# A graph network's second layer: weighted one-hots built by one comparison and one multiplication for four columns at once

## What is computed

```python
rel_w = jnp.einsum('rb,bio->rio', w_comp, weight)      # 8 relations
xw = jnp.einsum('ni,rio->rno', x, rel_w)
msg = xw[etypes, src] * norm                           # norm: one weight per edge
node_repr = jax.ops.segment_sum(msg, dst, num_segments=x.shape[0])
return jax.nn.relu(node_repr + h_bias)
```

## Time and profile before

| | us |
|---|---|
| time, median of 3 runs | 4172.07 |
| lowest and highest | 4169.52, 4172.36 |
| span of the profiled execution | 5935.9 |
| of it before the first gather | 78.5 |
| layer 0, first gather to last | 78.5 to 3291.9 |
| layer 1, first gather to last | 3384.6 to 5916.2 |

### The profile page before, as it was taken

How to read it: one execution, slowest core, us unless ns; L and a number is a source line. 1 busy time by engine, 2 the same in 40 slices (tenths; PEclk the granted TensorE clock), 3 DMA queues, 4 the chain that set the end, 5 groups by cost and what they waited for, 6 DMA issues and landing times.

```text
span 5935.9 us, 56570 instructions
## 1 busy us (share of the span) xinstructions
PE 2543.7 (43%) x11571; PEld 1919.2 (32%) x11572; DVE 1618.6 (27%) x4105; ACT 590.2 (10%) x1461; POOL 2977.3 (50%) x3193
## 2 busy tenths in 40 slices
PE   6555555445445555555454523333332332233323
PEld 5443443333333433333333322222222222222222
DVE  3222222222222322222222322223222222322323
ACT  2111111111111111111121200000000000000000
POOL 4455554544434444443434166665656555555554
PEclk7677676766666666666666555555555555555555
DMA  4411111111111111111111111111111111111111
GB/s 84 34 29 29 32 28 36 29 23 39 26 34 35 27 35 37 34 34 36 24 43 23 44 23 23 22 23 23 22 22 23 23 22 22 22 23 21 23 22 21
DMA packets 243962, 173.98 MB, mean 29 GB/s; under 512 B 127029, under 2 KB 179500, under 8 KB 243524
## 3 DMA queue, kind: packets, MB, share of 16 engines
q0 software_dynamic: 100096, 102.60, 9.7%
q1 hardware_dynamic: 142546, 67.57, 4.8%
q10 hardware_dynamic: 882, 0.13, 0.0%
HBM read 136.38 MB, written 33.70 MB: 29 GB/s over the span
## 4 chain that ended last, share of the span: by engine, by line
issue 34%; DVEq 20%; another core or an unknown queue 17%; PE 15%; DVE 12%; ACT 2%; ACTq 0%; DMA 0%; POOL 0%; POOLq 0%; SPq 0%
DVEq L879 5%; PE ps_agg L1217 4%; DVE work L936 3%; DVEq L936 3%; PE ps_fin L1289 3%; PE ps_o L1209 3%; DVEq L899 3%; DVEq L898 2%; DVE hid L948 2%; DVEq L913 2%; PE ps_z L1197 2%; PE ps_o L1205 1%; ACT acc L681 1%; DVE work L955 1%
## 5 line engine op out<-in xcount | busy, mean ns | idle before, releaser
L555 POOL DMA_INDIRECT rows<-node_table,src_ix x1564 | 1478.7, 945 | 1739.0 <-DVE work L955 1206.0
L555 POOL DMA_INDIRECT rows<-rel_table,src_ix x1564 | 1477.0, 944 | 1147.3 <-issue 460.3
L936 DVE TENSOR_SCALAR work<-ps_x,rel,enorm 128x128 f32<-128x128 f32 x1564 | 552.4, 404 | 912.7 <-issue 905.9
L1205 PE MATMUL ps_o<-b2e,ones 3*128 3x256 bf16 x391 | 134.6, 344 | 1379.2 <-DVE hid L948 1154.8
L1217 PE MATMUL ps_o<-work,rows 128*64 128x128 f32 x1248 | 291.4, 410 | 854.5 <-DVE work L936 529.0
L1217 PE MATMUL ps_agg<-work 128*64 128x128 f32 x3128 | 571.5, 342 | 47.5 <-issue 45.9
L899 DVE TENSOR_TENSOR acc<-acc,ps_agg 64x128 f32 x548 | 152.4, 278 | 1566.8 <-remote 981.8
L1217 PEld LDWEIGHTS ps_o<-work,rows 128*64 128x64 f32 x1248 | 234.3, 215 | 910.3 <-DVE work L936 555.4
L1205 PEld LDWEIGHTS ps_o<-b2e,ones 3*128 3x128 bf16 x391 | 37.4, 96 | 1485.9 <-DVE hid L948 1203.8
L1217 PEld LDWEIGHTS ps_agg<-work 128*64 128x64 f32 x3128 | 455.6, 175 | 154.1 <-issue 147.2
L1217 PE MATMUL ps_agg<-work,rows 128*64 128x128 f32 x1256 | 291.8, 412 | 342.8 <-DVE work L936 212.2
(11 more groups left out here) (137 smaller groups left out, 1905.6 us busy)
## 6 DMA issues: line engine op xcount, KB each, us to landing
rows<-node_table,src_ix POOLq DMA_INDIRECT x1564
rows<-rel_table,src_ix POOLq DMA_INDIRECT x1564
attr<-in_edge_attr_dram SPq DMA_DIRECT2D x78, 320.0 KB
rel_table<-acc SPq DMA_DIRECT2D x13, 1792.0 KB, 6.6
node_table<-work SPq DMA_DIRECT2D x24, 128.0 KB, 2.0
out_dram<-x_sb SPq DMA_DIRECT2D x13, 224.0 KB
rel_table<-acc SPq DMA_DIRECT2D x7, 256.0 KB, 2.0
src_ix<-row_groups SPq DMA_DIRECT2D x78, 10.0 KB
```

Of the source, the lines that this page charges most:

```text
L555: nc.gpsimd.indirect_dma_start(rows[0:n, slot_of(u), j, :], None, table, bass.IndirectOffsetOnAxis(ap=src_ix[0:n, half_of(u), col : col + ...
L936: last = nc.vector.tensor_scalar(o[:, j, :], iota_ps, r[:, j : j + 1], weights[:, j : j + 1], ALU.is_equal, ALU.mult)
L1205: nc.tensor.matmul(ps_o[u % 2][:, 0 : J * F], ones_3[:], b2e_3[:], start=True, stop=False, skip_group_check=True)
```

## The change

Layer 1's one-hots of a tile are made in two steps, each over 128x512 elements. `mark1` compares, with the same `one_hot` that layer 0 uses, and lifts a new semaphore `hot_marked`. `weigh1` waits for it, multiplies the tile's one-hots in place by the weights in `enorm`, repeated along the 128 places, and lifts `hot_ready`. `weigh1` of a tile stands behind `mark1` of the tile after it. So when VectorE gets to the sum of tile u, tile u+4 is marked and tile u+3 is weighted. The rare extra windows of a tile (`extras`) still use `weighted_hot`.

```diff
-            def prepare1(i, u):
-                s = tile_of(i, u)
-                weighted_hot(onehot[:, u % AHEAD, :, :], rel_of(s), s).then_inc(hot_ready, 1)
+            def mark1(i, u):
+                one_hot(onehot[:, u % AHEAD, :, :], rel_of(tile_of(i, u))).then_inc(hot_marked, 1)
+
+            def weigh1(i, u):
+                hot = onehot[:, u % AHEAD, :, :]
+                weights = enorm[:, bass.ds(tile_of(i, u), 1), :].rearrange("p o (j n) -> p (o j) n", n=1)
+                dve.wait_ge(hot_marked, tile_of(i, u) + 1)
+                nc.vector.tensor_tensor(hot, hot, weights.to_broadcast([P, J, P]), ALU.mult).then_inc(hot_ready, 1)
...
-            for u in range(AHEAD - 1):
-                prepare1(0, u)
+            mark1(0, 0)
+            for u in range(1, AHEAD - 1):
+                mark1(0, u)
+                weigh1(0, u - 1)
             with dve.Fori(0, BODIES - 1) as i:
                 for u in range(BODY):
-                    prepare1(i, u + AHEAD - 1)
+                    mark1(i, u + AHEAD - 1)
+                    weigh1(i, u + AHEAD - 2)
                     add_supertile1(i, u)
```

More of the change, by code:

```diff
@@ L281, in bass_gnn_resnorm_d2_kernel @@
         msg_ready = sem("msg_ready")
+        hot_marked = sem("hot_marked")
         hot_ready = sem("hot_ready")
@@ L1094, in _ @@
                 if u + AHEAD - 1 <= BODY:
-                    prepare1(BODIES - 1, u + AHEAD - 1)
+                    mark1(BODIES - 1, u + AHEAD - 1)
+                if u + AHEAD - 2 <= BODY:
+                    weigh1(BODIES - 1, u + AHEAD - 2)
                 add_supertile1(BODIES - 1, u, u == BODY)
```

## The result

The changed kernel takes 4207.60 us (median of 4 runs, 4201.21 to 4215.24) against 4172.22 us (4 runs, 4169.52 to 4174.0). The ratio is 1.0089, with a 95% interval of 1.0077 to 1.0101. The forecast was 4244 us, slower.

What follows compares the result with a forecast made beforehand. POOL's gathers were taken to bound both layers, at 5.0 us a tile. VectorE's work and the added wait cost 0 and collisions 72 us, so 4172 + 72 = 4244 us, range 4170 to 4330 us.

Steps and rivals of the forecast that it cites:

- The sum of POOL's steps: Both layers: 3127 gather steps of 1.249 us plus start, ring, between-layer and end terms, 4143.7 us, 0.7% below measured.
- The full ring: Layer 0's start: POOL fills the ring before the first message is made, 48.5 us more than a step.
- The long steps of 2.45 us: POOL's gathers: steps twice as long without a wait; one in every 80 gathers would be 47 us.
- The pace of 0.70 us: VectorE's sequencer in layer 1: about 0.70 us an instruction in slow stretches, taken as an effect of the recording.
- VectorE's own part: Layer 1: two instructions, together 1.37 us, replace four of 1.36 us; about 2.4 us a tile beside POOL's 5.0, cost 0.
- The added wait and the lag: Layer 1: wait on `hot_marked` met before reached, one-hots ready three tiles ahead instead of four; cost 0.
- The collision: Layer 1: the two-SBUF-input multiplication holds gathers at their reading point, 0.185 us a tile, 72 us; chance 0.72.
- the free phase: Layer 1: multiplication falls freely in POOL's 1.249 us step; collision chance 0.54, mean wait 0.34 us.
- No collision: Rival, layer 1: the weighings miss POOL's reading points or the held gather had another cause; 4172 us, chance 0.16.
- the whole length lost: Rival, layer 1: each multiplication costs POOL its full 0.68 us, 266 us, giving 4438 us; chance 0.08.
- Faster: Rival: VectorE bounds parts of layer 1, so fewer instructions bring back up to 28 us, 4144 us; chance 0.04.
- the gather at 2021.08: POOL's gather started 0.15 us after L1009 (SBUF with SBUF): 1.29 us instead of 0.945, 0.34 us lost.

Runs made afterwards that it cites:

- 128x768 between: The changed kernel with an idle 128x768 multiplication, one input in PSUM, between comparison and multiplication in the loop: 4211.19 us, ratio 1.0105.
- 128x256 between: The changed kernel with an idle 128x256 multiplication, one input in PSUM, between comparison and multiplication in the loop: 4176.82 us, ratio 1.0027.

## Why the prediction was right, and where not

**What bounds the kernel: right in layer 1, with a wrong reason, and in layer 0 partly by luck.** The sum of POOL's steps came to 4144 us. On a chip that isn't paced the terms can now be read, in the changed kernel: 79.4 us ahead of the first gather (78.5 assumed), 93.7 between the layers (92.7), 17.3 from the last gather's start (19.7). Layer 1 takes 1992.7 us from first to last start, that is 1563 steps of 1.249 us, 1952.2, and 40.5 more, which is what the held gathers lost. In layer 0 two errors partly cancel. The full ring cost 20.7 us more than a step and not the 48.5 that were read from the paced profile:

```profile
151.77 0.94 POOL L556 DMA_INDIRECT rows<-node_table,src_ix  x1 [20.98 <-DMA src_ix<-src_groups]
```

In its place seven later waits of POOL in layer 0, of 1.3 to 17.3 us, five of them put down to row numbers, cost 52.7 us beyond the usual step, and the sum had none of them. What is left of the two, 25 us, is most of the 28 us that the sum lacked. So layer 0 isn't bound by POOL's steps alone. These seven waits are about as large in the kernel before with the PSUM multiplication added (48.4 us), so they have nothing to do with the change. The long steps of 2.45 us, offered for the missing 28 us, don't appear there as a series: layer 1 has none. The pace of 0.70 us was put down to the recording. It goes with the chip that the run falls on: there all executions of the kernel before take 5839 to 5958 us, while profiles from the other chips don't show it. What causes it stays open. The waits that it makes were rightly left out for the chips of 4170 us, and would have been wrongly left out for the others.

**VectorE's own part at cost 0: right.** The comparison took 691 ns and the multiplication 682, as taken from L889 and L863. The run with the added multiplication from PSUM shows that 0.7 us a tile more on VectorE is free (ratio 0.9995).

**The added wait and the lag at cost 0: not refuted.** `hot_marked` shows up in no wait. The run without the lag fell on paced chips, so the lag's own price at POOL's pace was not measured; since 41.8 us of lost gathers stand against 35.4 us of lost time, there is hardly room for one.

**The collision: right in kind, too large in size.** This was the term that carried the forecast, read from one case in one trace, and 123 cases followed it. The term was 0.185 us a tile, 72 us; measured were 0.107 us, 41.8 us in the gathers and 35.4 us in the time, half of the forecast. It was mis-sized in two places:
- The hold was taken as long as the instruction's record, 0.68 us. It lasts 0.555. The earlier trace rows would have told: the gather was let go about 0.50 us after a 448-column instruction began, 0.13 us before its record ended. I had laid that 0.13 us on the gather's side, as the time until it reads; the lengthened multiplications at a gather's start show that it reads within some 0.05 us. With 0.555 us the free phase gives 391 x 0.555² / (2 x 1.249) = 48 us.
- The phase was taken as free. It is not: 31% of the multiplications held a gather, by 0.34 us, where a free phase would have 44%, by 0.28. Fewer collisions, each a little longer, left 42 of the 48 us. That they came so near to the free phase is luck: the run with 128x256 between lost 14 us.

**The rivals.** No collision and the whole length lost are out, the second because a gather that is past its start is seldom held, and 0.107 us a tile is far from 0.68. Faster is out: nothing came back. One argument for the collision was misread: of the four long gathers before 97 us none has VectorE reading SBUF "with both hands". Three ran beside casts, with one tensor input, and one beside a clearing, with none. Only the gather at 2021.08 ran beside an instruction with two SBUF inputs, so it alone bore the term. What the Trainium skill's "SBUF — State Buffer" says in "Who interferes with whom" of two SBUF inputs against a reading GpSimd instruction agrees with the runs here that had two SBUF inputs, and with the two that read one of them from PSUM and held nothing. That the later of the two is blocked shows both ways, in the 123 held gathers and in the 13 lengthened multiplications, but the gather was let go 0.13 us before the multiplication's record ended. The section infers that a `tensor_tensor` doesn't hold up the making of descriptors. For these gathers it can't be concluded from this that the multiplication is free: 57.4 us were lost in the run with the added multiplication in SBUF. Whether the reading of the row numbers or the making of the descriptors is held, no run here tells apart.

**The profile's signs.** A mean of 0.99 us was expected, 0.970 came; single gathers of up to 1.6 us, 1.458 came. Layer 0's mean stayed at 945 ns. The fall of the profiled span from 5936 to 4210 us came with the chip as far as the runs can tell, and says nothing for or against what was said of it.

## What to carry to other kernels

When POOL issues indirect DMAs back to back and is the bound, an instruction of VectorE is only free if it leaves POOL alone: keep one of two tensor inputs in PSUM, as the run that marked in PSUM did, or keep the instruction short, since at a free phase the loss goes with the square of its length (57 and 198 us for 512 and 1024 columns). Look through the durations of the bound engine's instructions for the few that stand out, and for what ran beside them: here one gather in 3128 held the answer. Take the time it was held from there, not from the other instruction's duration, and don't expect the phase between two engines to be random: a shift of 0.33 us changed the loss from 42 to 14 us.

## What the runs showed of the hardware

- A multiplication of 512 or 1024 columns with both inputs in SBUF held a gather until 0.555 or 1.088 us after its start, to within 14 ns. The same with 512 columns and an input in PSUM held none in 380 tiles, though 215 gathers started under it.
- A gather is nearly always past harm once it has started: in the changed kernel's trace 250 multiplications began 0.03 to 0.70 us into a gather, and neither they nor the gathers were lengthened. In the run with 128x768 between, five such gathers were held, four of them by a multiplication 0.23 us into them.
- A gather that starts within some 0.03 us of a multiplication can win: 13 multiplications of the changed kernel's trace took 0.698 to 0.749 us in place of 0.681, beside gathers of 0.94 us.
- On two of the four chips that the experiments ran on, the kernel before took 5855 and 5950 us in place of 4167 to 4170, with instructions of VectorE's sequencer at 0.7 us in stretches (970 of 0.65 to 0.76 us in the first profile of the kernel before, 2 in that of the changed kernel). Each chip was used at one time only, so the chip and the time aren't told apart. On those two the two-step one-hots without the lag were 0.2 to 0.3% faster than the kernel before; neither that run on the other two nor the changed kernel itself on these was timed.
